# GRU in a GNN kernel: the recurrent loop's body holds ten steps instead of two

## The reference

```python
pre_i = x_seq @ W_ih.T + b_ih
def step(h, pi):
    ph = h @ W_hh.T + b_hh
    r = sigmoid(pi[:H] + ph[:H])
    z = sigmoid(pi[H:2*H] + ph[H:2*H])
    n = tanh(pi[2*H:] + r * ph[2*H:])
    h_new = (1.0 - z) * n + z * h
    return (h_new, h_new)
_, ys = jax.lax.scan(step, zeros(H), pre_i)      # H = 512, 1250 steps
```

## Time and profile before

| | |
|---|---|
| three timed runs | 5081.4, 5085.2, 5091.0 us (median 5085.2) |
| profiled execution | 5089.8 us, its span 5087.7 us |
| PE busy | 4957.9 us, 97% of the span |
| mean granted clock of PE | 0.986 |
| GRU loop | from 699 to 3951 us |

### The profile page before, as it was taken

The page is one execution under the profiler, slowest core; times in us unless marked ns, Lnnn a source line. Parts: engine busy times, 40 slices in busy tenths (PEclk is TensorE's granted clock), DMA queues, the critical chain, the costliest instruction groups (busy, mean ns, idle before and its releaser), DMA issues.

```text
span 5087.7 us, 337016 instructions
## 1 busy us (share of the span) xinstructions
PE 4957.9 (97%) x131794; PEld 4250.1 (84%) x131795; DVE 2880.4 (57%) x16350; ACT 1950.7 (38%) x15372; POOL 846.6 (17%) x5071
## 2 busy tenths in 40 slices
PE   7899999999999999999999999999999999999989
PEld 7765579999999999999999999999999445555554
DVE  6551346666666666666666666666666525445551
ACT  0111025555555555555555555555555101222110
POOL 0000012222222222222222222222222000000000
PEclk9999999999999999999999999999999998999989
DMA  1011210000000000000000000000000100011011
GB/s 61 0 70 68 102 38 0 0 0 0 0 0 0 0 0 0 0 0 0 0 0 0 0 0 0 0 0 0 0 0 0 59 17 19 18 36 36 22 51 42
DMA packets 28932, 81.11 MB, mean 16 GB/s; under 512 B 1594, under 2 KB 1834, under 8 KB 28858
## 3 DMA queue, kind: packets, MB, share of 16 engines
q1 hardware_dynamic: 28858, 80.03, 4.3%
HBM read 58.08 MB, written 21.95 MB: 16 GB/s over the span
## 4 chain that ended last, share of the span: by engine, by line
PE 94%; DVE 2%; issue 2%; DVEq 1%; ACT 0%; POOL 0%; DMA 0%; ACTq 0%; SPq 0%; POOLq 0%
PE psum L494 64%; PE psum L567 8%; PE psum L363 5%; PE psum L353 4%; PE psum L579 4%; PE psum L411 3%; PE psum L476 2%; PE psum L553 2%; PE psum L643 2%; DVE r L880 1%; PE psum L426 0%; PE psum L458 0%; DVEq L875 0%; DVE r L879 0%; DVE stat L813 0%
## 5 line engine op out<-in xcount | busy, mean ns | idle before, releaser
L494 PE MATMUL psum<-h,r 128*128 128x16 f16 (+1 forms) x80000 | 3063.3, 181 | 9.1 <-ACT psum L707 4.3
L494 PEld LDWEIGHTS psum<-h,r 128*128 128x128 f16 x80000 | 2670.6, 96 | 39.1 <-DVEq L993 4.9
L494 PE MATMUL psum<-h,hn 128*128 128x16 f16 (+1 forms) x40000 | 2122.2, 177 | 0.0
L494 PEld LDWEIGHTS psum<-h,hn 128*128 128x128 f16 x40000 | 1592.6, 96 | 0.0
L999 DVE TENSOR_TENSOR_SCAN psum<-mul_rz,psum 128x6 f32<-128x6 f32 x5000 | 854.9, 171 | 590.8 <-PE psum L494 542.5
L707 ACT COPY psum<-big 128x2 f32 (+1 forms) x7506 | 1002.8, 163 | 0.0
L315 POOL TENSOR_TENSOR upd_add<-upd,signs 128x4 f32<-128x4 f32 x2500 | 504.2, 202 | 2591.2 <-DVE upd L1018 1832.0
L720 ACT ACTIVATE mul_n<-psum 128x2 f32<-128x2 f32 x2500 | 434.4, 174 | 1177.9 <-DVE psum L999 1177.8
L1018 DVE TENSOR_TENSOR_SCAN upd<-upd_mul,upd_add 128x8 f32<-128x8 f32 x2500 | 417.2, 167 | 300.4 <-ACT upd_mul L725 300.4
L729 ACT ACTIVATE upd_add<-psum 128x2 f32<-128x2 f32 x2500 | 434.1, 174 | 297.4 <-DVE psum L1005 297.4
L1014 DVE TENSOR_TENSOR_SCAN h<-upd_mul,upd_add 128x8 f16<-128x8 f32 x2500 | 425.2, 170 | 169.9 <-POOL upd_add L315 3.8
(11 more groups left out here) (224 smaller groups left out, 2538.1 us busy)
## 6 DMA issues: line engine op xcount, KB each, us to landing
ws<-in_Wl SPq DMA_DIRECT2D x9, 1024.0 KB, 5.4
ws<-in_Wr SPq DMA_DIRECT2D x9, 1024.0 KB, 7.6
edge_counts<-adj SPq DMA_DIRECT2D x2, 3051.8 KB
edge_weights<-big SPq DMA_DIRECT2D x1, 6103.5 KB
adj_rows<-big SPq DMA_DIRECT2D x1, 6103.5 KB
adj<-adj_rows SPq DMA_DIRECT2D x1, 6103.5 KB
big<-edge_counts SPq DMA_DIRECT2D x1, 6103.5 KB
adj<-edge_weights SPq DMA_DIRECT2D x1, 6103.5 KB
```

What stands on the lines that cost most here:

```text
L494: m = mm(places, whh16[g][:, part, 2 * kc + k, (2 * c + j) * P:(2 * c + j + 1) * P], state.unsqueeze(1).broadcast_to([P, COPIES, 2 - part] ...
```

## The change

A constant `STEPS = 10` takes the place of the 2 in all four loops. The loop turns 125 times, its body is written out for ten steps, and `u` is the parity of the step within the body. The work of a step and its order are the same.

```diff
+STEPS = 10
...
-            with pool.Fori(0, N // 2) as i:
-                for u in range(2):
-                    t = 2 * i + u
+            with pool.Fori(0, N // STEPS) as i:
+                for step in range(STEPS):
+                    t = STEPS * i + step
+                    u = step % 2
                     for c in range(2):
                         pool.wait_ge(s(f"gru_high{c}"), t + 2)
...
-            with pe.Fori(0, N // 2) as i:
-                for u in range(2):
-                    t = 2 * i + u
+            with pe.Fori(0, N // STEPS) as i:
+                for step in range(STEPS):
+                    t = STEPS * i + step
+                    u = step % 2
                     pe.wait_ge(s("gru_high0"), t + 1)
```

More of the change, by code:

```diff
@@ L713, in _ @@
                 put(0, 1, g).then_inc(s(f"gru_put_{'rzn'[g]}1"), 1)
-            with act.Fori(0, N // 2) as i:
-                for u in range(2):
-                    t = 2 * i + u
+            with act.Fori(0, N // STEPS) as i:
+                for step in range(STEPS):
+                    t = STEPS * i + step
+                    u = step % 2
                     def gate_r(c):
@@ L1028, in low_part @@
                 v.tensor_tensor(h16[:, 1 - u, c, 7:16:8], upd[:, 1 - u, c, 3:8:4], h16[:, 1 - u, c, 6:16:8], ALU.subtract).then_inc(s(f"gru_low{c}"), 1)
-            with dve.Fori(0, N // 2) as i:
-                for u in range(2):
-                    t = 2 * i + u
+            with dve.Fori(0, N // STEPS) as i:
+                for step in range(STEPS):
+                    t = STEPS * i + step
+                    u = step % 2
                     made = nc.vector.compute_val(t + 2)
```

## The result

The kernel after takes 6216.7 us (median of 5 runs, 6210.6 to 6223.5), the one before 5085.2 us: a ratio of 1.222, with a 95% interval of 1.2205 to 1.2241. The forecast was 5860 us, range 5470 to 6250; the sign and the mechanism came as forecast. The loss was 1131 us and not 775, which is 33 us inside the top of the range.

A forecast was written before the change was run, and what follows sets the result against it. PE (TensorE) was taken to bound the GRU loop, working without a stop inside a step. The terms summed to 6.2 us per trip, times 125 = 775 us more, giving about 5860 us; range 5470 to 6250.

The forecast's parts named there:

- Term 1: GRU loop on PE: four of five branches go, 0.13 us each, 65 us less in all.
- Term 2: PE's loop branch: reading the target's instruction block takes 3.3 us, 3.1 us more per trip than a branch that hits.
- Term 3: PE, block after the target's: asked for only on entering the target's 32 instructions, so 2.9 us more per trip.
- Term 4: PE, seven other block reads per trip: 3.3 us each, hidden behind 3.46 us of work, so 0; 0.6 at 3.54.
- Term 5: PE after its stops: granted clock falls to the lower level, costing 0.7 us per trip.
- the sign that term 4 is wrong: Profile after, PE in the GRU loop: stops at each block, 128 pairs apart.
- it fits: Rival, PE's instruction memory: PE keeps 10 blocks or more, so only branches are saved, about 5020 us; chance 0.11.
- Only the target misses: Rival, PE's loop branch: the block behind the target comes along or is held; 381 us more, about 5470; chance 0.07.
- The reads cannot keep pace: Rival, PE's block reads: each of seven stops PE 1.8 us more, 22.8 us per trip, about 7900 us; chance 0.04.
- The other engines' branches at nothing: DVE, ACT and POOL loops: their branches stand in idle time, so removing them is worth nothing.

The follow-up runs named there:

- Experiment 3: Kernel before with eight steps in PE's loop body, two steps behind the loop, other engines kept at two: 5039.7 us, ratio 0.9915.
- experiment 4: Kernel before with eight steps on PE and 20 instructions of waits ahead of PE's loop: 5335.3 us, ratio 1.050.
- experiment 5: Kernel before with eight steps on PE and 31 instructions of waits ahead of PE's loop: 5815.5 us, ratio 1.144.
- experiment 7: Kernel before with ten steps on PE and 110 instructions ahead of PE's loop: 5797.8 us, ratio 1.1405.
- experiment 8: Kernel before with fifty steps in PE's loop body, 25 trips: 5528.5 us, ratio 1.087.
- experiment 6: Kernel before with ten steps on PE and 32 instructions ahead, so the branch's target starts a block: 5718.7 us, ratio 1.125.
- experiment 2: Kernel before with ten steps on DVE, ACT and POOL, PE kept at two: 5086.4 us, ratio 1.000.

## Why the prediction was right, and what it mis-sized

The chain of reasons held: the new body does not stay, and every trip reads it again, with two long stops at the branch. PE's body needs 10 blocks counting the one ahead, and each trip had 10 packets. Experiment 3 has 8 blocks that stay, 4 and 5 have 9 that don't always: PE keeps eight blocks of 256. The prediction had that number only between 4 and 16, so that ten blocks would not stay was a judgement and not a reading. The Trainium skill ("Runtime: NRT & Kernel Launch", Instruction fetch mechanics) gives 2048 instructions for PE, which is these eight blocks; its other statement, that the memory is only two lines, does not hold for PE in these runs. The new body's 1942 instructions are fewer than 2048 and still don't fit, since whole blocks count and one is taken by the read ahead.

By its terms, per trip of ten steps (a gap here is the time from the start of one matmul to the start of the next, and the figures are means over the trips unless said otherwise):

- Term 1, the branches: 0.13 us each was too much; it is 0.093 by the steps of experiment 3. The statement that a step without a branch runs at 2.53 us was read from the one step that follows a branch; in a row they take 2.55. Four branches: 0.4, not 0.5.
- Term 2, the target's block: 3.1 forecast. The median gap at the branch is 4.20 us against 0.15 before: 4.0. The price of 3.3 us for a lone read was somewhat low (the branch took 3.5 to 3.6 us in experiments 7 and 8), but the larger part is that the branch comes while the read ahead, asked for when the last block was entered 118 instructions earlier, is still on its way (experiments 6 and 7). The prediction counted that block among the ten that must be held, but not among its 9 packets per trip, and gave it no price.
- Term 3, the block behind: 2.9 forecast, 2.6 measured, and experiment 6 shows that it is what it was said to be.
- Term 4, the other blocks: 0 forecast, "the cover is thin", 0.6 with its dearer price. This is the largest error. There is no stop at the first of the seven later block ends, which PE reaches at the lower clock; the stops at the other six add 2.15 us, 0.36 each, and experiment 8 confirms it apart from the branch. The term took 3.3 us for a read against 3.46 of work; the packets follow each other in 3.4 to 4.1 us. The stops at the block ends are what the prediction had named as the sign that term 4 is wrong.
- Term 5, the clock: 0.7 forecast. What the other terms leave of the trip is 0.7.

Sum: 4.0 + 2.6 + 2.15 + 0.7 - 0.4 = 9.1 us, times 125 = 1140, against 1131 measured and 775 forecast. Of the 2.9 us per trip that were missing, term 4 has 2.15 and term 2 0.9, and term 3 gives 0.3 back. The range held because its upper end had every read at 3.8 us.

Of the rivals, "it fits" needed ten blocks and there are eight. "Only the target misses" fell by the packets: after a miss all blocks are read again, not those alone that were pushed out. "The reads cannot keep pace" came true in kind but not in size: 0.36 us at a block end, where it had 1.8. The other engines' branches at nothing was right (experiment 2).

## What to carry to other kernels

Count a loop body in instruction blocks, from where it begins in its block and with the block that is read ahead, for the engine with the most instructions; on PE each matmul is two. Up to eight blocks of 256, a longer body saves about 0.09 us per branch. With nine, from some to all of the branches missed here, by where the body ended in its last block (experiments 4 to 7); with ten or more, all did. A trip that misses pays 3.3 to 4.9 us at the branch, a second stop where few instructions stand behind the target in its block (2.6 us with 32), and 0.2 to 0.4 us on average for each further block, with PE at 27 ns a pair. Leave a block to spare: in experiment 4, 20 instructions outside the loop cost 296 us. In the profile, look at packets of the instruction queue inside a loop, and at the branch's duration.

## What I had not expected

- Losing the blocks can be a matter of a few instructions between a block's end and the branch: 27 losses in 156 trips at 6 instructions, 77 at 17, and every trip at 150 and 228 (there with ten steps in the body).
- A loss costs all blocks, about 9 packets and 10 to 11 us, though only one block too many was touched.
- Straight-line code can run faster than its instructions come: at 27 ns per pair of load and matmul, PE stopped 0.36 us on average at each of 37 blocks in a row, with no other DMA traffic.
